# The last group of a GRU and ternary FFN kernel: eight hidden tiles kept on chip, the down products moved behind all gate and up products

## What is computed

```python
def cell(h, x):
    gi = x @ W_ih + b_ih
    gh = h @ W_hh + b_hh
    r = sigmoid(i_r + h_r); z = sigmoid(i_z + h_z)
    n = tanh(i_n + r * h_n)
    return (1 - z) * n + z * h            # 32 steps, one after the other

gate, up = split(hs @ ternary(w_gate_up).T)   # 2 x 1024 columns for each token
h = silu(gate) * up                           # 1024 hidden values per token
h = h * rsqrt(mean(h * h) + eps)
out = x + h @ ternary(w_proj).T               # 256 outputs per token
```

## Time and profile before

| what | value |
|---|---|
| median of three runs | 346.06 us |
| the profiled execution's own time | 346.3 us |
| its span, first to last instruction | 344.5 us |
| mean granted clock of the tensor engine | 1.000 |
| PE busy | 339.4 us, 99% of the span |
| DVE busy | 233.6 us, 68% |
| ACT busy | 222.8 us, 65% |
| POOL busy | 184.0 us, 53% |
| last group, from its first gate product to the end of the span | 314.5 to 344.5 us |

### The profile page before, as it was taken

One profiled execution on the slowest core, in us unless ns is written; L12 is line 12 of the kernel. 1 busy time (PEld: TensorE's weight loads), 2 busy tenths in 40 slices (PEclk: granted clock), 3 DMA queues, 4 the chain that ended last, 5 costly groups with the idle time before them and its releaser, 6 DMA issues.

```text
span 344.5 us, 5631 instructions
## 1 busy us (share of the span) xinstructions
PE 339.4 (99%) x2059; PEld 295.2 (86%) x2059; DVE 233.6 (68%) x462; ACT 222.8 (65%) x438; POOL 184.0 (53%) x156
## 2 busy tenths in 40 slices
PE   8999999999999999999999999999999999999996
PEld 4889988788988889888888889888888888888895
DVE  7578788899677565755667554875558555664866
ACT  5768888886756757555766656566564655756662
POOL 2315571465825446255454446444472554799694
PEclk9999999999999999999999999999999999999999
DMA  7994000045001000140001000010000100010101
GB/s 240 319 410 192 3 0 2 0 148 220 1 2 62 2 0 0 44 142 2 0 0 63 0 2 0 2 63 0 2 0 2 60 1 2 0 64 1 57 6 61
DMA packets 7891, 18.72 MB, mean 54 GB/s; under 512 B 564, under 2 KB 4788, under 8 KB 7352
## 3 DMA queue, kind: packets, MB, share of 16 engines
q1 hardware_dynamic: 7176, 17.97, 13.9%
q10 hardware_dynamic: 688, 0.39, 0.4%
HBM read 14.17 MB, written 4.19 MB: 53 GB/s over the span
## 4 chain that ended last, share of the span: by engine, by line
PE 94%; DVE 3%; ACT 1%; issue 1%; DVEq 0%
PE ps_ffn L1105 30%; PE ps_out L1143 16%; PE ps_rz L1017 7%; PE ps_rz L1022 7%; PE ps_rz L1018 7%; PE ps_n L1017 3%; PE ps_n L1022 3%; PE ps_n L1018 3%; PE ps_rz L1105 2%; PE ps_ffn L1270 2%; PE ps_t L1098 1%; PE ps_ffn L1017 1%; PE ps_ffn L1022 1%; PE ps_ffn L1018 1%; PE ps_n L1055 1%
## 5 line engine op out<-in xcount | busy, mean ns | idle before, releaser
L354 POOL TENSOR_TENSOR hid_lo<-work,hid_hi 128x512 fp32r<-128x512 f32 x62 | 81.7, 1317 | 103.6 <-ACT hid_hi L452 99.6
L1105 PE MATMUL ps_ffn<-st_hi,wguT 128*128 128x512 f32 x236 | 93.7, 397 | 0.3 <-DVE work L737 0.3
L1105 PE MATMUL ps_ffn<-st_lo,wguT 128*128 128x512 f32 x236 | 92.7, 393 | 0.0
L361 POOL TENSOR_TENSOR sq_sum<-sq_sum,work 128x512 f32<-128x512 f32 x55 | 73.2, 1331 | 1.8 <-ACT work L466 0.6
L737 DVE TENSOR_TENSOR work<-work,ps_ffn 128x512 f32<-128x512 f32 x55 | 37.6, 683 | 31.5 <-ACT work L448 31.5
L452 ACT CAST hid_hi<-work 128x512 fp32r<-128x512 f32 x63 | 38.8, 616 | 23.0 <-DVE work L747 23.0
L1105 PEld LDWEIGHTS ps_ffn<-st_hi,wguT 128*128 128x128 f32 x236 | 44.4, 188 | 8.3 <-DVE work L737 0.9
L1105 PEld LDWEIGHTS ps_ffn<-st_lo,wguT 128*128 128x128 f32 x236 | 44.5, 189 | 7.3
L747 DVE TENSOR_TENSOR work<-work,ps_ffn 128x512 f32<-128x512 f32 x63 | 43.2, 686 | 4.7 <-PE ps_ffn L1105 2.8
L1143 PEld LDWEIGHTS ps_out<-wpT,hid_hi 128*128 128x128 f32 x240 | 35.8, 189 | 3.7
L1143 PE MATMUL ps_out<-wpT,hid_lo 128*128 128x256 f32 x240 | 38.8, 284 | 0.0
(11 more groups left out here) (226 smaller groups left out, 716.0 us busy)
## 6 DMA issues: line engine op xcount, KB each, us to landing
out_dram<-o_st SPq DMA_DIRECT2D x7, 512.0 KB, 2.6
xT_all<-in_x_dram SPq DMA_DIRECT2D x1, 3072.0 KB, 17.6
x_ring<-in_x_dram SPq DMA_DIRECT2D x1, 3072.0 KB, 11.5
x_ring<-in_L_ffn_w_gate_up_dram SPq DMA_DIRECT2D x4, 512.0 KB, 8.9
x_ring<-in_L_ffn_w_proj_dram SPq DMA_DIRECT2D x2, 512.0 KB, 11.6
x_ring<-in_x_dram SPq DMA_DIRECT2D x1, 1024.0 KB, 5.4
work<-in_L_cond_W_ih_dram SPq DMA_DIRECT2D x3, 256.0 KB, 4.4
work<-in_L_cond_W_hh_dram SPq DMA_DIRECT2D x3, 256.0 KB, 4.6
```

The lines of the kernel that those rows point to most:

```text
L354: nc.gpsimd.tensor_tensor(hid_lo[:, j % RING], hid[:, j % 2], f32(hid_hi[:, j % RING]), ALU.subtract).then_inc(hid_lo_ok, 1)
L361: nc.gpsimd.tensor_tensor(sq_sum[:], sq_sum[:], hid_sq[:, j % 2], ALU.add).then_inc(sq_added, 1)
L1105: mm = pe.matmul(bank, w, group_state(part, G, k), start=(k == 0 and i == 0), stop=(k == KD - 1 and i == 1))
```

## The change

Only the last group (G = 7) is changed. Its order on the PE becomes: all gate and up products (the items C6, C7 and S of the group before stay where they were), then the high down products of tiles 0 to 7, then one set of token squares (the ordinary `token_squares`, eight matmuls in f32), then the low down products of tiles 0, 1, 4 and 2 for all time steps, and last, time step by time step, those of tiles 5, 3, 6 and 7. Tile 7 is a whole tile again. All eight tiles of `hid`, of high parts and of low parts have places of their own, in memory that the recurrence no longer needs, so `hidden` doesn't wait for squares and low parts of earlier tiles. Two output rows lie in `ps_out` banks, two in `ps_n` and in the bank of gate 6.

POOL makes the low parts of tiles 0, 1, 2 and 3 and adds all seven squares, tile 7's too; DVE makes the low parts of tiles 4 (right behind `hidden` of tile 6), 5, 6 and 7 (behind `hidden` of tile 7). ACT's stream of tiles 3 to 7 keeps the pattern sigmoid j, high part j - 1, square j - 1, and ends with square 7 and high part 7. Each output row is stored by itself.

```diff
-PE_END = [..., "G4", "D0", "D1", "U4", "D2", "G5",
-          "U5", "D3", "G6", "U6", "D4", "Ga", "Ua", "Gb", "Ub", "D5", "H6", "T0", "T2", "Ta", "Tb", "L0", "L2"]
+PE_END = [..., "G4", "U4", "G5", "U5", "G6", "U6",
+          "G7", "U7"]
...
+        late = xT_all[:].rearrange("p k t b -> p (k t b)").rearrange("p (i c) -> p i c", c=512)
+        free = [w[:].rearrange("p k n -> p (k n)").rearrange("p (i c) -> p i c", c=512) for w in (wi_hi, wi_lo, wh_hi, wh_lo)]
+        spare = [w[:, i] for w in free for i in range(3)] + [hid_lo[:, i] for i in range(RING)]
+        def hid_of(G, j):
+            return late[:, j] if is_late(G) else hid[:, j % 2]
+        def hi_of(G, j):
+            return spare[j] if is_late(G) else hid_hi[:, j % RING]
+        def lo_of(G, j):
+            return spare[HT + j] if is_late(G) else hid_lo[:, j % RING]
+        last_out = (ps_out[:, 0, :], ps_out[:, 2, :], ps_n[:, 0:D], gate_bank(NG - 1, HT - 2)[:, 0:D])
+        POOL_LOWS, DVE_LOWS = (0, 1, 2, 3), (4, 5, 6, 7)
...
-            for first, last in ((0, 2), (2, 3)):
-                sp.wait_ge(o_last, last)
-                sp.dma_start(out[:, T - GS + first:T - GS + last, :], o_st[:, first:last, :]).then_inc(stored, 16)
+            for s in range(GS - 1):
+                sp.wait_ge(o_last, s + 1)
+                sp.dma_start(out[:, T - GS + s, :], o_st[:, s, :]).then_inc(stored, 16)
...
+            G = NG - 1
+            pool.wait_ge(limb_3, G)
+            low_part(G, 0)
+            finish(G - 1)
+            low_part(G, 1)
+            for j in range(1, HT):
+                add_square(G, j)
+                if j in (2, 4):
+                    low_part(G, 1 + j // 2)
+            finish(G)
...
+                act.wait_ge(hid_ok, 8 * G + j + 1)
+                nc.scalar.activation(hid_sq[:, j % 2], hid_of(G, j), ACT.Square).then_inc(hid_sq_ok, 1)
...
+            hidden_square(G, HT - 1)
+            hidden_hi(G, HT - 1)
             act.wait_ge(o_last, GS)
...
-                if n >= 2:
+                if n >= 2 and not is_late(G):
                     dve.wait_ge(hid_sq_ok, n - 1)
                     dve.wait_ge(hid_lo_ok, n - 1)
...
+                    if is_late(G) and j == HT - 2:
+                        low_part(G, DVE_LOWS[0])
+            for j in DVE_LOWS[1:]:
+                low_part(NG - 1, j)
+            mean_square(NG - 1)
             rows_out(NG - 1)
...
             for item in PE_END:
                 ffn_item(NG - 1, item)
+            pe.wait_ge(o_ok, NG - 1)
+            pe.wait_ge(gsg_ok, HT * NG - 1)
+            for j in range(HT):
+                late_down(hi_of, j)
+            token_squares(NG - 1)
+            for j in (0, 1, 4, 2):
+                late_down(lo_of, j)
+            for s in range(GS):
+                for j in (5, 3, 6, 7):
+                    mm = late_down(lo_of, j, (s,))
+                mm.then_inc(down, 1)
```

More of the change, by code:

```diff
@@ L208, in up_bank, with is_late, low_number @@
             return product_bank(product(G, j, "up"))
[L210 to L216, removed]
+        late = xT_all[:].rearrange("p k t b -> p (k t b)").rearrange("p (i c) -> p i c", c=512)
+        def is_late(G):
+            return G == NG - 1
+        free = [w[:].rearrange("p k n -> p (k n)").rearrange("p (i c) -> p i c", c=512) for w in (wi_hi, wi_lo, wh_hi, wh_lo)]
[8 more added lines that the diff above has]
+        POOL_LOWS, DVE_LOWS = (0, 1, 2, 3), (4, 5, 6, 7)
+        def low_number(j):
+            return 8 * (NG - 1) + POOL_LOWS.index(j) + 1 if j in POOL_LOWS else DVE_LOWS.index(j) + 1
         def state(parts, t):
@@ L459, in hidden_square @@
                         act.wait_ge(sq_tok, G)
-                    nc.scalar.activation(sq_sum[:], hid[:, 0], ACT.Square).then_inc(hid_sq_ok, 1)
+                    nc.scalar.activation(sq_sum[:], hid_of(G, 0), ACT.Square).then_inc(hid_sq_ok, 1)
                     return
@@ L470, in hidden_parts @@
                 hidden_square(G, j)
[L472 to L486, removed]
             def first_limb(G):
@@ L651, in _ @@
                 hidden_parts(G, 1)
-                for j in range(3, HT if G < NG - 1 else HT - 2):
+                for j in range(3, HT):
                     silu_part(G, j)
@@ L753, in mean_square @@
                                         ALU.add).then_inc(ms_ok, 1)
[L755 to L758, removed]
             def rows_out(G):
-                dve.wait_ge(down, G + 1)
+                if not is_late(G):
+                    dve.wait_ge(down, G + 1)
                 dve.wait_ge(inv_ok, G + 1)
@@ L766, in rows_out @@
                 for s in range(GS):
-                    if G == NG - 1 and s == 2:
-                        dve.wait_ge(down, NG + 1)
-                        dve.wait_ge(inv_ok, NG + 1)
+                    if is_late(G):
+                        dve.wait_ge(down, G + 1 + s)
                     last = nc.vector.scalar_tensor_tensor(
-                        out=o_st[:, s, :], in0=ps_out[:, s, :], scalar=inv[:, s:s + 1],
+                        out=o_st[:, s, :], in0=last_out[s] if is_late(G) else ps_out[:, s, :], scalar=inv[:, s:s + 1],
                         in1=x_ring[:, (GS * G + s) % XR, :], op0=ALU.mult, op1=ALU.add)
@@ L1132, in down_product @@
                     pe.wait_ge(q_mean_ok, NU)
[L1133 removed]
+                elif j == 0 and G == NG - 2:
                     first_down(G)
@@ L1180, in token_squares @@
                 mm.then_inc(sq_tok, 1)
[L1182 to L1194, removed]
@@ L1196, in down_part, with late_down @@
-            def down_part(part, ok, j, steps):
-                if j == HT - 1 and part is hid_lo:
-                    pe.wait_ge(lo_last, 1 if steps[0] == 0 else 2)
+            def late_down(part, j, steps=range(GS)):
+                G = NG - 1
+                if part is hi_of:
+                    pe.wait_ge(hid_hi_ok, 8 * G + j + 1)
                 else:
-                    pe.wait_ge(ok, 8 * (NG - 1) + j + 1 + (j == HT - 1 and steps[0] > 0))
+                    pe.wait_ge(hid_lo_ok if j in POOL_LOWS else lo_last, low_number(j))
@@ L1201, in down_part @@
                 for s in steps:
-                    mm = pe.matmul(ps_out[:, s, :], part[:, j % RING, s * P:(s + 1) * P], wpT[:, j, :],
-                                   start=False, stop=part is hid_lo and j == HT - 1, skip_group_check=True)
-                return mm
-            def last_high():
-                for first in (0, 2):
-                    down_part(hid_hi, hid_hi_ok, HT - 2, (first, first + 1))
-            def last_rows(s):
-                steps = (s, s + 1)
-                down_part(hid_hi, hid_hi_ok, HT - 1, steps)
-                down_part(hid_lo, hid_lo_ok, HT - 2, steps)
-                down_part(hid_lo, hid_lo_ok, HT - 1, steps).then_inc(down, 1)
@@ L1218, in last_squares @@
-            def last_squares(part):
-                steps = (0, 1) if part in ("0", "a") else (2, 3)
-                first = part in ("0", "2")
-                if part == "0":
-                    pe.wait_ge(ms_ok, NG - 1)
-                    pe.wait_ge(sq_added, 7 * NG - 1)
-                elif part == "2":
-                    pe.wait_ge(hid_ok, HT * NG - 1)
-                else:
-                    pe.wait_ge(sq_last, 1 if part == "a" else 2)
-                squares = sq_sum[:] if first else hid_sq[:, 1]
-                for s in steps:
-                    mm = pe.matmul(last_sq[s // 2][:, s % 2:s % 2 + 1], squares[:, s * P:(s + 1) * P], ones[:],
-                                   start=first and s % 2 == 0, stop=not first, skip_group_check=True)
-                if not first:
-                    mm.then_inc(sq_tok, 1)
+                    mm = pe.matmul(last_out[s], part(G, j)[:, s * P:(s + 1) * P], wpT[:, j, :],
+                                   start=j == 0 and part is hi_of, stop=False, skip_group_check=True)
@@ L1247, in ffn_item @@
                 kind, which = item[0], item[1:]
-                if kind == "T":
-                    last_squares(which)
-                elif kind == "H":
-                    last_high()
-                elif kind == "L":
-                    last_rows(int(which))
-                elif which in ("a", "b"):
-                    last_product(which, "gate" if kind == "G" else "up")
-                elif kind == "G":
+                if kind == "G":
                     gate_product(G, int(which))
```

75 lines of the change are left out of this document (13 added, 62 removed).

## The result

The changed kernel takes 350.51 us (median of four runs, 349.48 to 351.03), the kernel before 346.06: a ratio of 1.0118, 95% interval [1.0102, 1.0134]. Forecast were 348.2 and a range of 346.9 to 349.2. The direction was right, the size was not: +4.45 us instead of +2.1. The profiled execution took 351.02 us with a span of 349.2, against 346.3 and 344.5 before. The mean granted clock of the tensor engine was 1.000 in the profile before; in the four runs of the changed kernel it was 0.990, 0.995, 0.990 and 0.994, for 351.02, 350.00, 351.03 and 349.48 us.

The account below looks back on a forecast made before the run. POOL's additions, ending at 338.71, were taken to release the squares; squares 0.89, low products 3.80, 0.17 to leave the array and DVE's 0.53 gave 344.25 against 342.06, +2.19, so 348.2 us against 346.06. Range 346.9 to 349.2.

Parts of the forecast that it names:

- What bounds the end: Last group: POOL never idles from addition 2 on, its last addition ends at 338.71, and the PE's squares wait for it.
- What is taken away: Last group: squares in one set gain 0.89, tile 7 whole 0.08, one last DVE row instead of two 0.45; together 1.42.
- U4's wait: PE, up product of tile 4: waits 0.88 for its bank, which DVE's hidden of tile 2 reads; covered by POOL's chain.
- POOL's chain with the port: Eight POOL operations from 327.10 end at 337.76; three turns with DVE at the shared port add 0.95, giving 338.71.
- High part 7: ACT makes it behind square 7, ending near 336.5; the PE waits 0.8 before the eighth high product; covered by POOL's chain.
- the squares' wait: PE ahead of the token squares: it is there 1.8 us before POOL's last addition ends at 338.71.
- The sum, +2.19: Span: squares begin at 338.86; 0.89, 3.80 and 0.17 of PE work, then DVE's 0.53, end at 344.25, before 342.06.
- (c): Rival missing from the prediction as given; the reflection puts its clock part at 348.9 to 352.9; whole rival's chance 0.13.
- (a): Rival: the port between DVE and POOL costs nothing, 348.2 - 0.95 = 347.3; chance 0.15.
- (b): Rival: not slower, POOL releases the squares before the PE is there at 336.2; 345.5, or 344.6; chance 0.12.

Follow-up runs that it names:

- u4_free: Changed kernel with filling matmuls in both late PE gaps (two and six) and tile 4's up product in the free bank ps_n: 348.30 us, ratio 1.0053.
- port_free: Changed kernel with filling matmuls in both PE gaps (two and four) and DVE's low parts held until the last addition is done: 347.45 us, ratio 1.0030.

## Why the prediction was wrong, step by step

- **What bounds the end** (POOL's additions, which the PE must wait for): right. The PE waits 1.43 us at the squares for POOL's `sq_sum`, and POOL doesn't stand idle between addition 2 and the last.
- **What is taken away** (1.42 us): the squares' 0.89 is 0.92 at the full clock, the last row ends 0.52 behind the PE (347.00 - 346.48). Right.
- **U4's wait**: 0.82 for 0.88, and covered, as far as u4_free shows.
- **POOL's chain with the port**: 11.53 for 11.61; the port's share 0.92 for 0.95 by port_free, with a turn costing 0.45 ahead of low part 3, which doesn't wait for the addition before it, and 0.24 between two additions (the forecast had 0.44 and about 0.25). None of these turns cost POOL the full 0.69 of a DVE operation.
- **High part 7**: wait 0.62 for 0.8, and the squares' wait 1.43 for 1.8; the forecast left out the 0.17 until the last matmul ends, and the squares begin 0.06 behind the last addition, not 0.15.
- **The sum, +2.19**: this is the step that failed. It set behind the last addition 0.89 + 3.80 + 0.17 us of PE work at durations read at the full clock, although the same sum had the PE idle 0.8 and 1.8 us right in front. In the changed kernel it is 1.49 + 6.55. With the idle time filled the time is 348.19, against 348.2 forecast; that it fits to 0.01 is luck, as small misses above and below cancel. The missing term was the clock: 350.51 - 348.19 = 2.3 us, or 2.0 by the ratios.
- **The rivals**: the clock stood there as a part of (c), at 348.9 to 352.9, and the result lies in it. Its price there, the 4.7 us behind taking twice as long, was too high: they took 3.1 more, since the clock fell when the squares had begun and was back before the end, and since a step from matmul to matmul grew from 0.24 to 0.43 for two, less than double. The step of judgement that failed was to give all of (c) a share of 0.13, and to reason from a profile in which the clock never fell: behind the first 1.45 us its list of waits has only one of the PE, 0.3 us, so that profile could say nothing for a clock that holds through a wait near the end. With that the range ended at 349.2, where it should have reached past 350. The other rivals fell: (a) by port_free, (b) by the gap at the squares. The other parts of (c), a second turn for DVE or a dearer one, fell by POOL's chain of 11.53.

## What to carry to other kernels

A wait of the tensor engine near the end can cost more than its length: price the matmuls behind it at the low clock too, as a case of its own, wherever the profile of before has no idle time to read the answer from. Before many products are collected behind one gate, look at what opens the gate, here a chain of additions on POOL with no slack; work that doesn't need the gate goes in front of it. And when a chain is shortened, ask which engine's stream the next small step (a mean, a power) is queued in.

## What the runs showed of the hardware

- After idle stretches of 0.62 and 1.43 us, with 0.73 us of work in the 2.00 from 336 to 338, the clock fell from 2.4 to 1.2 GHz near 338.7; it stayed down for some 6.8 us though the PE was busy throughout, to about 345.5. With the short stretch filled, which left 1.44 us and little else, it fell about 2 us later and was down for some 3.4 us (340.7 to 344.1), and in one run of four it didn't fall. With the long one filled and 0.60 left it held in all four runs. U4's wait of 0.82, with the PE busy in front of it and behind, didn't bring it down in any trace that has it.
- Useless bf16 matmuls in the gaps kept it up, and cost nothing: six of 512 columns took 1.47 us and ended at 338.63, before the last addition did (338.71).
- In the last group DVE operations with two SBUF inputs and POOL's took turns wherever they met. A turn that DVE takes makes POOL's next operation 0.45 longer (1.74 for 1.29), for a DVE operation of 0.69; between two additions of which one waits for the other it costs 0.24 (4.62 for 4.14, two turns). A DVE operation that must wait for its turn took up to 1.76.
